# Rebuilding the opening stage of a two-layer conditioned FFN kernel on one core

## The chip, the cores and the metric

The kernel runs on one core of one Trainium2 chip, in one launch. The metric is device time in microseconds; the three runs of the kernel before gave 229.94, 229.96 and 230.28 us, with a median of 229.96 us. All inputs are drawn at random and are float32.

## The reference, cut to what matters

`x` is 32 samples of 32 channels by 512 positions, and `c = cond_128` is 32 by 128. Two layers follow each other, each with a conditioning part and an FFN part, each added to its input:

```python
# layer 0, conditioning: grouped conv over the positions, plus one number for each (sample, channel)
out  = conv1d(x, weight, groups=4, kernel=9) + (c @ c_weight.T)[:, :, None] + fside[None, :, None]
# layer 0, FFN
shared = relu(out @ up_w)**2 @ down_w
s      = top2(out @ gate_w).sum(-1)
routed = ((out @ fc1_w) @ expert_w) * s @ fc2_w
x = x + layernorm(shared + routed) * gamma + beta
# layer 1, conditioning: attention over 8 kernels, one 32x32 matrix and one bias row for each sample
h = gelu(c @ W0 + b0); h = gelu(h @ W1 + b1); att = softmax(h @ W2 + b2)
agg_w = einsum('bk,koi->boi', att, weight); agg_b = att @ bias_k
y = einsum('boi,bih->boh', agg_w, x) + agg_b[:, :, None]
# layer 1, FFN: dense W plus eight low-rank experts, weighted by a softmax of q.k
x = x + y @ W.T + b + combined(softmax(q.k), y @ A, Bm)
```

## The kernel before, in words

The work is tiled into 8 tiles (T = 0 to 7) of four samples each, 128 rows of 512 positions; layer 0 works in two halves (h = 0, 1) of four tiles. The program is written by hand: each engine has its own list of instructions, in order, and semaphores are the only order between engines. Almost every product of the FFN is done as three fp32r matmuls (`mm3`, L1121 to L1123) on operands split into a high part (made by ScalarE) and a low part (made by VectorE, for some weights by GpSimd); a float32 matmul shows as two passes in the trace.

Opening, in TensorE's order: the conv weights are turned into `wconv` (transposes at L1293; VectorE writes the mask product `wc_pad` before it at L907 and the copy out of PSUM after it at L913); the conditioning rows are turned into `cT` and `cwT` (L1299, L915); `conv(0)` and `conv(1)` (L1133); `turn_expert` (L1283); two `ones_r` matmuls on each half of `prod0` that give `B0`, the conditioning number of every (sample, channel) on all 128 partitions (L1313); the first layer of the attention MLP (L1318); `conv(2)`, `conv(3)`; the second MLP layer; the fold of `expert_w` and `fc2_w` into one matrix `ex` by twelve `mm3` matmuls (L1121 to L1123 with operands `ex_lo`, `dn_lo`); the logits (L1337). Then the up chunks begin.

For a conv of tile T, VectorE and ScalarE first make shifted copies of `x` in `XS` (`shift_copies(i)`: part 0 is tile 0, part 1 is tile 1, part 2 is tiles 2 and 3, part 3 is the second half; VectorE does 10 of 16 pieces of a part, ScalarE 6; L437, L438). `add_ctx(T)` (L808) adds `B0` to the conv result; `split_H(T)` makes `H_hi` (ScalarE L618) and `H_lo` (VectorE L818), the operands of the up chunks. `split_up(c)` makes the parts of up chunk c (ScalarE L609, VectorE L798). `B0` comes from `prod0` on GpSimd (L520), its split (ScalarE L663, VectorE L920), and an add of `fsb`, the side vector, on VectorE (L929). GpSimd's two large memsets, `gate_hl` and `BD`, stand behind `prod0` in its list (L523, L524).

A half h: up chunks 0 and 1 on the first two tiles, chunk 0 on the other two, `gate_rows`, chunk 1 on the other two, `gate_logits`, up chunk 2 (it waits for `s_R`, the split of chunk 0's squared result, L849), `scale_rows` (it waits for `diag`, VectorE L839 and ScalarE L640), two `latent`, and then eight down chunks with `up(c+3)` between them. In half 0 the transposed attention (`turn_att`, L1341), `mixing` (the 32x32 matrices of all samples, L1349) and `mixing_bias` (L1359) stand between the up chunks; VectorE turns the matrices (L979) and GpSimd writes them into the block-diagonal `BD` (L543). `mix(T)` (L1243) uses `BD` in the last down chunks of half 1 and after. Half 1 begins with `conv(4)` to `conv(7)`.

SyncE issues nearly all loads in one list: x part 0, `c_nat`, x parts 1 and 2, `fsb`, `exraw`, seven small tensors of the attention MLP, `wk`, `fc2`, `gate`, the first half of `up_raw`, `fc_raw`, the second half, two halves of `dn_raw`, x part 3, `gamma`, `rowb`, and 32 block loads of the q and k weights. ScalarE's queue carries two loads, `wc_nat` and `cw_nat`.

## Time and profile before

| | |
|---|---|
| median of three runs | 229.96 us |
| the profiled execution: its span | 228.5 us |
| TensorE matmul busy | 217.1 us, 95% |
| VectorE busy | 134.6 us, 59% |
| ScalarE busy | 85.0 us, 37% |
| GpSimd busy | 62.0 us, 27% |
| the chain that ended last, by engine | PE 87%, DVE 9%, DMA 1%, ACT 1% |
| DMA engines, mean busy share in the first eighth of the span | 0.5 to 0.9 and above |

The profiler's page gives for the profiled execution its span alone; the median of the runs lies 1.46 us above that span, and this difference is taken as what lies around the program. PE is TensorE, PEld its weight loads, DVE is VectorE, ACT is ScalarE, POOL is GpSimd, SP is SyncE, and an engine's name with a q is its queue of issued DMAs. "Idle before" in a row is the time for which an engine had nothing to do ahead of that group, with what ended it.

### The profile page before, as it was taken

The page shows a single profiled execution, that of the slowest core. Times are in us where ns is not written, and L with a number is a line of the kernel's source. Part 1 is how long each engine was busy: PE and PEld are TensorE (multiplying, and loading weights), DVE is VectorE, ACT ScalarE, POOL GpSimd, SP SyncE. Part 2 cuts the span into 40 slices and gives each one's busy share as a digit, 9 for nine tenths or more (in the row PEclk, how much of TensorE's full clock was granted, in tenths as well). Part 3 has the DMA queues.
Part 4 walks back from the last instruction along what each step waited for, and adds up shares of the span by engine and source line. Part 5 has one row for each costly group of instructions (what it writes and reads, how often), then busy time and mean ns, then how long its engine had stood idle before and what let it go on. Part 6 is the DMA issues. An engine that isn't in the chain of part 4 may idle for free.

```text
span 228.5 us, 3173 instructions
## 1 busy us (share of the span) xinstructions
PE 217.1 (95%) x1181; PEld 186.1 (81%) x1181; DVE 134.6 (59%) x279; ACT 85.0 (37%) x165; POOL 62.0 (27%) x72
## 2 busy tenths in 40 slices
PE   2787999999999999999999999999999999999994
PEld 2777886788788888999888888888998998999982
DVE  4998589876943334957462113445997555435442
ACT  6946576745954441123531013442112211211110
POOL 2504022545146643206300002442262220122000
PEclk9999999999999999999999999999999999999999
DMA  5999944200000000007526000000000110110103
GB/s 141 258 392 390 317 59 68 34 0 0 0 3 0 0 0 0 3 0 116 84 35 75 17 3 1 0 0 0 3 0 0 46 49 0 47 46 3 46 4 135
DMA packets 30400, 13.56 MB, mean 59 GB/s; under 512 B 24936, under 2 KB 25512, under 8 KB 30384
## 3 DMA queue, kind: packets, MB, share of 16 engines
q1 hardware_dynamic: 30288, 13.33, 22.2%
q8 instruction: 9, 0.15, 0.3%
q14 instruction: 7, 0.06, 0.1%
q10 hardware_dynamic: 96, 0.03, 0.1%
HBM read 11.26 MB, written 2.10 MB: 58 GB/s over the span
## 4 chain that ended last, share of the span: by engine, by line
PE 87%; DVE 9%; DMA 1%; ACT 1%; issue 0%
PE PS L1121 25%; PE PS L1122 25%; PE PS L1123 24%; PE PS L1133 7%; DVE XS L437 5%; PE PS L1243 3%; DVE up_lo L798 2%; DMA wc_nat<-in_L_cond_weight_dram 1%; DVE H_lo L920 1%; DVE dn_lo L972 0%; ACT fc_hi L690 0%; PE PS L1147 0%; PE PS L1146 0%; PE PS L1272 0%; PE PS L1359 0%
## 5 line engine op out<-in xcount | busy, mean ns | idle before, releaser
L845 DVE TENSOR_TENSOR PS<-PS,relu 128x512 f32<-128x512 f32 x16 | 11.1, 693 | 32.4 <-ACT relu L624 32.4
L1121 PE MATMUL PS<-H_hi,up_hi 128*128 128x512 f32 (+1 forms) x80 | 28.3, 354 | 0.0
L1122 PE MATMUL PS<-H_lo,up_hi 128*128 128x512 f32 (+1 forms) x80 | 27.9, 349 | 0.0
L1123 PE MATMUL PS<-H_hi,up_lo 128*128 128x512 f32 (+1 forms) x80 | 27.8, 347 | 0.0
L1133 PE MATMUL PS<-wconv,XS 128*128 128x128 f32 x192 | 25.0, 295 | 2.0 <-DVE wconv L913 1.5
L1133 PEld LDWEIGHTS PS<-wconv,XS 128*128 128x128 f32 x192 | 24.3, 210 | 2.5 <-DVE wconv L913 1.6
L1121 PE MATMUL PS<-qkT_hi,H_hi 128*128 128x320 f32 x64 | 20.3, 317 | 0.1
L1122 PE MATMUL PS<-qkT_lo,H_hi 128*128 128x320 f32 x64 | 19.8, 309 | 0.0
L1123 PE MATMUL PS<-qkT_hi,H_lo 128*128 128x320 f32 x64 | 19.8, 309 | 0.0
L624 ACT ACTIVATE relu<-PS 128x512 f32<-128x512 f32 x16 | 9.5, 597 | 25.1 <-PE PS L1123 25.1
L570 POOL TENSOR_TENSOR X<-X,rowb 128x512 f32<-128x512 f32 x8 | 10.3, 1288 | 31.3 <-PE PS L1243 31.3
L437 DVE COPY XS<-X 32x128 f32<-32x128 f32 (+2 forms) x40 | 18.1, 454 | 0.5
L1122 PE MATMUL PS<-dn_lo,ring 128*128 128x512 f32 x44 | 17.5, 399 | 0.0
L1121 PE MATMUL PS<-dn_hi,ring 128*128 128x512 f32 x44 | 17.4, 396 | 0.0
L1121 PEld LDWEIGHTS PS<-H_hi,up_hi 128*128 128x128 f32 x80 | 15.1, 189 | 2.7 <-issue 0.4
L1123 PE MATMUL PS<-dn_hi,ring 128*128 128x512 f32 x44 | 17.3, 392 | 0.0
L1123 PEld LDWEIGHTS PS<-H_hi,up_lo 128*128 128x128 f32 x80 | 15.1, 189 | 2.1
L1122 PEld LDWEIGHTS PS<-H_lo,up_hi 128*128 128x128 f32 x80 | 15.1, 189 | 2.0
L438 ACT ACTIVATE XS<-X 32x128 f32<-32x128 f32 (+2 forms) x24 | 15.8, 658 | 0.6 <-DMA X<-in_x_dram 0.3
L532 POOL TENSOR_TENSOR dn_lo<-dn_raw,dn_hi 128x512 fp32r<-128x512 f32 x8 | 10.3, 1289 | 17.2 <-ACT dn_hi L613 17.2
L574 POOL TENSOR_TENSOR wT_lo<-qk_raw,wT_hi 128x512 fp32r<-128x512 f32 x4 | 5.1, 1292 | 36.2 <-ACT wT_hi L658 36.2
L1121 PE MATMUL PS<-wT_hi,H_hi 128*128 128x512 f32 x32 | 13.1, 409 | 0.0
(189 smaller groups left out, 476.5 us busy)
## 6 DMA issues: line engine op xcount, KB each, us to landing
up_raw<-in_L_ffn_up_w_dram SPq DMA_DIRECT2D x2, 1024.0 KB, 8.0
dn_raw<-in_L_ffn_down_w_dram SPq DMA_DIRECT2D x2, 1024.0 KB, 12.9
out_dram<-X SPq DMA_DIRECT2D x8, 256.0 KB, 2.0
X<-in_x_dram SPq DMA_DIRECT2D x1, 1024.0 KB, 15.2
XS<-in_L_ffn_W_dram SPq DMA_DIRECT2D x16, 64.0 KB, 2.3
X<-in_x_dram SPq DMA_DIRECT2D x2, 256.0 KB, 3.4
X<-in_x_dram SPq DMA_DIRECT2D x1, 512.0 KB, 5.4
fc<-in_L_ffn_fc_w_dram SPq DMA_DIRECT2D x1, 512.0 KB, 3.6
```

The lines of the kernel that those rows point to most:

```text
L437: return nc.vector.tensor_copy(dst, src)
L438: return nc.scalar.activation(dst, src, ACT.Copy)
L532: nc.gpsimd.tensor_tensor(dn_lo[:, c, :], dn_raw[:, c, :], dn_hi[:, c, :].bitcast(F32), ALU.subtract).then_inc(s_dn, 1)
L570: nc.gpsimd.tensor_tensor(X[:, T, :], X[:, T, :], rowb[:], ALU.add).then_inc(s_x1b, 1)
L574: nc.gpsimd.tensor_tensor(wg_dst(g, False), wg_turned(g), wg_dst(g, True).bitcast(F32), ALU.subtract)\
L624: nc.scalar.activation(relu[:], U[i % 2], ACT.Relu).then_inc(s_relu, 1)
L845: nc.vector.tensor_tensor(U[i % 2], U[i % 2], relu[:], ALU.mult).then_inc(s_sq, 1)
L1121: nc.tensor.matmul(o, lh, rh, start=start, stop=False)
L1122: nc.tensor.matmul(o, lh, rl, start=False, stop=False)
L1123: return nc.tensor.matmul(o, ll, rh, start=False, stop=stop)
L1133: last = nc.tensor.matmul(conv_bank(T)[:, s * P:(s + 1) * P], XS[:, T % TPH * SPT + s, a:a + P], wconv[:, a], start=(a == 0), stop=(a == N ...
L1243: last = nc.tensor.matmul(mix_bank(T)[:, p, :], X[:, T, p * P:(p + 1) * P], BD[:, T], start=True, stop=True)
```

## The change

Four things change together. (1) GpSimd no longer makes `prod0` or `fc2_lo`, so its memsets run at once. (2) The conditioning numbers: TensorE multiplies `cT` by `cwT` in float32 (32x32), VectorE adds `fs32`, the side vector, ScalarE's queue stores the 4 KB to DRAM (`ctx_rows`) and loads them back, broadcast to 128 partitions, as `B0` (512 KB). (3) The fold of `expert_w` and `fc2_w` is done by four float32 matmuls (`expert_latent`) instead of twelve fp32r ones with splits, between `conv(1)` and `conv(2)`; `turn_expert` goes ahead of `conv(0)`. (4) The attention MLP and the mixing move: MLP layers and logits to down chunks 1, 3 and 5 of half 0, the softmax to the end of half 0, `mixing_bias` and `mixing` between the convs of half 1, and their results go through DRAM (`aggb_rows`, `agg_rows`) into `B1` and `BD`. Six float32 matmuls on `ones` (`warm(6)`) stand at the head of TensorE's list. The order of the loads, of the shifted copies of part 0, and of the splits is changed with it.

```diff
@@ SyncE @@
             load_x(0)
-            sp.dma_start(c_nat[:], cond_128).then_inc(ld_c, 16)
+            sp.dma_start(exraw[:], L0_ffn_expert_w.rearrange("(c p) m -> p c m", p=P)).then_inc(ld_ex, 16)
             load_x(1)
+            sp.dma_start(fc2[:], L0_ffn_fc2_w.rearrange("(c p) l -> p c l", p=P)).then_inc(ld_fc2, 16)
             load_x(2)
-            sp.dma_start(fsb[:], fside_S_0.partition_broadcast(P)).then_inc(ld_fs, 16)
...
+            sp.dma_start(fs32[:], fside_S_0.partition_broadcast(N)).then_inc(ld_fs, 16)
...
+            sp.dma_start(wk[:], L1_cond_weight.rearrange("k o i a -> k o (i a)")).then_inc(ld_wk, 16)
+
+            sp.wait_ge(s_E2p, LC)
+            for dst, src in ((W0, L1_cond_W0), (W1, L1_cond_W1), (W2, L1_cond_W2), (bk, L1_cond_bias_k)):
+                sp.dma_start(dst, src).then_inc(ld_cond, 16)
...
+            sp.wait_ge(s_agg, 2)
+            sp.dma_start(agg_rows.rearrange("n i o -> n (i o)"), agg).then_inc(st_agg, 16)
+            sp.wait_ge(st_aggb, 16)
+            sp.wait_ge(st_agg, 16)
+            sp.dma_start(B1[:], aggb_rows.rearrange("n o -> (n o)").partition_broadcast(P)).then_inc(ld_B1, 16)
+            for s in range(SPT):
+                sp.dma_start(BD[C * s:C * (s + 1), :, C * s:C * (s + 1)], blocks[s]).then_inc(ld_BD, 16)
@@ GpSimd @@
-            pool.wait_ge(s_cT, 1)
-            nc.gpsimd.tensor_tensor(prod0[:], bcast_mid(cwT[:], N), cT[:].unsqueeze(2).broadcast_to([CD, N, C]),
-                                    ALU.mult).then_inc(s_prod0, 1)
-            nc.gpsimd.tensor_tensor(fc2_lo, fc2[:], fc2_hi.bitcast(F32), ALU.subtract).then_inc(s_fc2, 1)
-            for s in range(SPT):
-                nc.gpsimd.tensor_copy(BD[C * s:C * (s + 1), :, C * s:C * (s + 1)],
@@ ScalarE @@
+            act.dma_start(c_nat[:], cond_128).then_inc(ld_c, 16)
...
-            for i in range(3):
-                shift_copies(i)
...
+            shift_copies(0)
+            act.wait_ge(s_wcT, 1)
+            nc.scalar.activation(wconv[:].rearrange("p a q -> p (a q)"), M[1][:, 0:NWIN * P], ACT.Copy)\
+                .then_inc(s_wconv, 1)
+            act.wait_ge(s_ctx, 1)
+            act.dma_start(ctx_rows, ctx_sb[:]).then_inc(st_ctx, 16)
+            shift_copies(1)
+            act.wait_ge(st_ctx, 16)
+            act.dma_start(B0[:], ctx_rows.rearrange("n o -> (n o)").partition_broadcast(P)).then_inc(ld_B0, 16)
             act.wait_ge(s_exTp, 1)
+            nc.scalar.activation(exT[:].rearrange("p c m -> p (c m)"), D[3], ACT.Copy).then_inc(s_exT, 1)
+            shift_copies(2)
+            split_up(0)
             split_H(0)
...
+            def mixing_rows():
+                for b in range(2):
+                    act.wait_ge(s_AGp, b + 1)
+                    nc.scalar.activation(agg[:, b * BANK:(b + 1) * BANK], M[b][0:N, :], ACT.Copy).then_inc(s_agg, 1)
@@ VectorE @@
-            shift_copies(0)
-            dve.wait_ge(s_wcT, 1)
-            nc.vector.tensor_copy(wconv[:].rearrange("p a q -> p (a q)"), M[1][:, 0:NWIN * P]).then_inc(s_wconv, 1)
+            dve.wait_ge(ld_x[0], 16)
+            for j in range(PH):
+                phase_copy(nc.vector, 0, j, *XPARTS[0])
+            for j in range(PH):
+                phase_copy(nc.vector, 1, j, *XPARTS[0])
             dve.wait_ge(s_cTp, 1)
             nc.vector.tensor_copy(cT[:], M[0][:, 0:N])
             nc.vector.tensor_copy(cwT[:], M[0][:, N:N + C]).then_inc(s_cT, 1)
+            for j in range(2):
+                last = phase_copy(nc.vector, 2, j, *XPARTS[0])
+            last.then_inc(xs_v, 1)
+            dve.wait_ge(ld_fs, 16)
+            dve.wait_ge(s_ctxp, 1)
+            nc.vector.tensor_tensor(ctx_sb[:], M[0][0:N, 2 * C:3 * C], fs32[:], ALU.add).then_inc(s_ctx, 1)
             shift_copies(1)
             shift_copies(2)
+            split_up(0)
             add_ctx(0)
@@ TensorE @@
                 if T == TPH + 2:
-                    pe.wait_ge(s_lat, LC)
+                    pe.wait_ge(s_agg, 2)
...
+            pe.wait_ge(s_ones, 1)
+            warm(6)
             pe.wait_ge(s_ident, 2)
...
+            turn_expert()
+            pe.wait_ge(s_cT, 1)
+            nc.tensor.matmul(M[0][0:N, 2 * C:3 * C], cT[:], cwT[:], start=True, stop=True).then_inc(s_ctxp, 1)
...
-            turn_expert()
...
+            expert_latent()
             pe.wait_ge(xs_v, 3)
             pe.wait_ge(xs_a, 3)
             conv(2)
             conv(3)
...
+                    conv(TPH)
+                    mixing_bias()
+                    conv(TPH + 1)
+                    mixing()
+                    conv(TPH + 2)
+                    conv(TPH + 3)
...
+                    if h == 0 and c == 1:
+                        hidden1()
+                    if h == 0 and c == 3:
+                        hidden2()
+                    if h == 0 and c == 5:
+                        logits()
+                if h == 0:
+                    turn_att()
```

The new `expert_latent` waits for `exT` and `fc2`, then runs, for each of two output banks, two float32 matmuls of 128x512, and raises `s_E2p`; `warm(n)` runs n float32 matmuls of 128x128 on `ones` into a PSUM bank that nothing reads.

## Rows read from the trace of the kernel before

**Rows 1.** The page's first part: busy time, share of the span and instructions.
```profile
PE 217.1 (95%) x1181; PEld 186.1 (81%) x1181; DVE 134.6 (59%) x279; ACT 85.0 (37%) x165; POOL 62.0 (27%) x72
```

**Rows 2.** Windows: stretch, its us, busy us (instructions) by engine, PEclk, DMA share, GB/s.
```profile
7.33:13.28 5.95, 5.48 (x24) 5.19 (x24) 5.77 (x13) 5.81 (x11) 3.38 (x4) 1.00 0.95 281
13.28:19.75 6.47, 4.61 (x34) 4.22 (x35) 5.96 (x13) 2.20 (x3) 1.35 (x1) 1.00 1.04 395
19.75:25.34 5.59, 5.59 (x54) 5.59 (x52) 4.13 (x7) 2.66 (x4) 1.03 (x1) 1.00 1.05 388
25.34:28.54 3.20, 3.20 (x18) 2.40 (x16) 2.09 (x6) 2.98 (x5) 0.00 (x0) 1.00 1.22 265
28.54:40.26 11.72, 11.55 (x71) 8.71 (x69) 10.88 (x21) 8.47 (x18) 2.95 (x2) 1.00 0.42 64
40.26:91.00 50.74, 50.74 (x220) 41.05 (x220) 29.26 (x48) 26.02 (x42) 23.62 (x22) 1.00 0.02 4
91.00:101.50 10.50, 10.50 (x96) 10.50 (x95) 8.65 (x15) 1.89 (x3) 1.49 (x4) 1.00 0.01 2
```

**Rows 3.** Waits of TensorE: who waited for whom, total us, times, longest.
```profile
PE PS L1313 <- DVE H_lo L920: 1.9, 1, 1.9
```

**Rows 4.** The chain of waits (start, us, what), then GpSimd's timeline over the same time.
```profile
7.78 3.23 DVE XS L437
...
7.55 1.99 POOL L520 TENSOR_TENSOR prod<-cwT,cT 128x1024 f32<-128x1024 f32 x1 [5.14 <-DVE cwT L916]
9.98 0.95 POOL L524 MEMSET BD<- 128x1024 f32 x1
```

**Rows 5.** VectorE: timeline (start, us, engine, line, operation), then one from the chain.
```profile
3.94 2.74 DVE L437 COPY XS<-X 32x128 f32<-32x128 f32 x10
...
13.26 0.39 DVE XS L437
```

**Rows 6.** ScalarE's timeline in the opening: shifted copies, small and large, a table load.
```profile
4.91 0.86 ACT L438 ACTIVATE XS<-X 32x128 f32<-32x128 f32 x2
9.53 1.99 ACT L438 ACTIVATE XS<-X 32x256 f32<-32x256 f32 x3
20.00 1.28 ACT L670 ACT_TABLE_LOAD   x1 [1.68 <-PE PS L1318]
```

**Rows 7.** SyncE's timeline (one issue); DMA issues (KB, us to landing); one window.
```profile
2.63 0.47 SPq L451 DMA_DIRECT2D fsb<-in_fside_S_dram  x1
...
X<-in_x_dram SPq DMA_DIRECT2D x1, 512.0 KB, 5.4
fsb<-in_fside_S_dram SPq DMA_DIRECT2D x1, 16.0 KB, 5.1
cw_nat<-in_L_cond_c_weight_dram ACTq DMA_DIRECT2D x1, 16.0 KB, 2.4
gamma<-in_L_ffn_ln_gamma_dram SPq DMA_DIRECT2D x1, 256.0 KB, 12.0
...
10.00:12.00 2.00, 2.00 (x12) 2.00 (x11) 1.95 (x5) 1.96 (x4) 0.93 (x2) 1.00 0.88 266
```

**Rows 8.** TensorE's timeline: the first MLP layer and the mixing, both float32.
```profile
19.62 0.30 PE L1318 MATMUL PS<-cT,W 128*128 128x32 f32 x2
...
33.24 1.90 PE L1349 MATMUL PS<-wk,attT 8*32 8x512 f32 x4
```

**Rows 9.** Timeline of VectorE, GpSimd and ScalarE ahead of up chunk 2 and scale_rows.
```profile
33.53 3.82 DVE L798 TENSOR_TENSOR up_lo<-up_raw,up_hi 128x512 fp32r<-128x512 f32 x3 [0.15 <-ACT up_hi L609]
...
33.06 2.54 POOL L528 TENSOR_TENSOR fc_lo<-fc_raw,fc_hi 128x1024 fp32r<-128x1024 f32 x1 [12.28 <-ACT fc_hi L690]
...
41.59 1.28 ACT L640 ACTIVATE lat_hi<-ident,ssum_lo 128x128 fp32r<-128x128 f32 x4 [1.81 <-DVE ssum_lo L837]
```

**Rows 10.** Timeline at the start of half 1: ScalarE's first split, VectorE's first norm.
```profile
95.87 0.63 ACT L618 ACTIVATE H_hi<-tf 128x512 fp32r<-128x512 f32 x1 [9.20 <-DVE tf L808]
...
89.00 0.70 DVE L882 BATCH_NORM_STATS2 st<-PS 128x6 f32<-128x512 f32 x1 [3.00 <-PE PS L1123]
```

More of the change, by code:

```diff
@@ L704, in _ @@
                 if h:
[L705 to L706 removed]
+                    split_H(TPH)
+                    mixing_rows()
+                    for T in range(TPH + 1, TILES):
+                        split_H(T)
                 up_relu(i0)
```

300 lines of the change are left out of this document (117 added, 183 removed).

## The prediction, made before the changed kernel ran

> **What bounds the kernel now.** I read the page's busy times first: TensorE is busy 217.1 of 228.5 us, so nothing moves the end but TensorE's own passes or its idle time [rows 1]. Then the windows, cut where TensorE's work changes [rows 2]. TensorE issues its first conv pass at 7.33 us and its first up matmul at 28.54 us. Between these lie four convs (96 passes), the turned expert weight, B0, the fold, and idle time: 0.5 us before 13.28 and 1.86 us in the stage to 19.75. From 28.54 on it is full (50.74 of 50.74 us in the window from 40.26 to 91, 10.50 of 10.50 in the convs of half 1 [rows 2]), with 0.17 us of idle ahead of 40.26. So a microsecond taken from TensorE's list, or from its waits ahead of 28.54, is a microsecond of the end, as long as no other engine becomes late. The waits name the large one: B0's matmul waits 1.9 us for the split of prod0 [rows 3]. The chain of waits names why VectorE was late for conv(1): one small shifted copy took 3.23 us, where its ten neighbours took 0.27 each, and it spans GpSimd's prod0 and its memsets, from 7.55 to 10.93 [rows 4, 5]. I read that as VectorE being held off by GpSimd.
>
> **Part 1, up to conv(0).** The memsets of gate_hl and BD (0.5 and 0.95 us [rows 4]) now run from about 2.4 to 3.9, so they can hold up the mask product at 3.36 by 0.6 us instead of a copy by 3. VectorE then makes 8 copies (2.2 us), cT and cwT (0.3), 2 copies (0.55): 4.0 + 0.6 + 3.05 = 7.65. ScalarE has one more DMA to issue (0.4), 6 copies at 0.43 (2.6 [rows 6]) and the wconv copy, 7.0. conv(0) starts near 7.75 instead of 7.33. conv passes cost 5.59 us for 48 in the fourth stage of rows 2, 0.117 each, and 5.48 for 24 in the second, 0.228 each: conv(0) ran at the lower of TensorE's two levels (1.2 GHz), though the PEclk column says 1.00, and conv(1) and all after it at 2.4. With warm(6) and the other early passes I expect the change of level inside conv(0), which ends at 10.5 to 13; it doesn't matter, for the next step is later.
>
> **Part 2, the wait for fs32.** This is what I expect to eat most of the opening's gain. In the new VectorE list the side vector is waited for ahead of shift_copies(1), and ScalarE waits for the result (s_ctx) ahead of its own shift_copies(1). fs32 is in SyncE's list behind x part 2, as fsb was, but exraw (256 KB) and fc2 (512 KB) have been put ahead of it. fsb was issued at 2.63 and landed 5.1 us later, at 7.73; x part 2, ahead of it, 5.4 us after its issue at about 2.15: they landed together, so SyncE's loads come home in order [rows 7]. At the 266 GB/s of the window from 10 to 12 us, 768 KB more are 2.95 us; at the 395 of the third stage, 2.0 [rows 2, 7]. The seven small loads no longer mix in. I take 2.5: fs32 at 10.25, between 9.7 and 10.7. Then: add 0.3 (10.55); ScalarE issues the store (0.45) and makes 6 copies (2.65): 13.7. VectorE's ten end at 13.3. conv(1) starts at 13.75, 0.5 us later than before. Queued behind the waiting instruction on VectorE are the 20 copies of parts 1 and 2, on ScalarE the store, 12 copies and the exT copy.
>
> **Part 3, conv(1) to the up chunks.** conv(1) 2.8 (16.55). The fold is right behind it: exT is copied by 14.8. It has no row in float32; the nearest is mixing, 1.90 us for 4 passes of 512 columns [rows 8], so 8 passes are 3.7 (bound below: fp32r passes of 12 in 3.20 us, 2.1 for 8; above, the lower level, 7.3; I take 3.7, the same kind of operation). It ends at 20.25, conv(2) and conv(3) at 25.85, where before the up chunks began at 28.54. Gain: 2.65 us. In other words, of TensorE's old list 1.9 of idle, 1.1 of B0, 0.6 of turn_expert and 0.3 of MLP go, 0.6 net is lost on the fold, 0.5 on the start.
> Beside it, who could be late: ScalarE, from 13.7, the B0 issue (0.45), exT (0.6), six large copies at 0.66 (4.0 [rows 6]) and split_up(0): 19.35. VectorE's large copies (10 at 0.39 [rows 5]) end at 17.2, its split_up(0) at 20.0. Then two add_ctx and two split_H, to 22.6, and split_up(1), to 23.2. The up chunks at 25.85 have 2.6 us to spare. B0 must be there at 20.0. It is issued on ScalarE's queue at 13.7 (the store, issued at 10.6, must have landed; cw_nat on that queue took 2.4 us while megabytes of SyncE's were queued [rows 7]). 512 KB at half of 390 GB/s are 2.7 us, and I add 1.5 of cw_nat's 2.4 us for the way there and back: 4.2, that is 17.9. Bounds: 2.4 us (that row) and 12 us (gamma, a broadcast in SyncE's own crowded queue). I take 4.2, by the row on ScalarE's queue.
> The Trainium skill (DMA: Bandwidth & Descriptors, on arbitration) says that each DMA engine takes turns between the queues of different issuers, packet by packet; cw_nat's 2.4 us against fsb's 5.1 agrees.
>
> **Part 4, up to scale_rows.** TensorE loses from the stage of 11.72 us [rows 2]: turn_att 0.12, mixing 1.85 [rows 8], mixing_bias and its wait 1.25. Gain: 3.2 us. But up(2) waits for VectorE's split of chunk 0, and here VectorE gets late. add_ctx(3) can only start when conv(3) ends, now just ahead of the up chunks and not 3.2 us ahead. From 25.85 (A): add_ctx(3), split_H(3), the gate's low part, two ex_lo: A + 3.3. Three split_up: 3.82 us as before, since GpSimd's fc_lo falls on them again [rows 9]: A + 7.1. Square, ScalarE's split, VectorE's split: A + 9.2. TensorE is ready for up(2) at A + 11.72 - 3.2 - 0.17 = A + 8.35. Stall: 0.9 us (0.3 if fc_lo misses them, 1.5 if ex_lo slips). Likewise scale_rows waits for the diagonals: 1.95 us of small operations and 1.28 [rows 9] behind that split, against 2.8 of up(2): 0.45.
>
> **Part 5, what comes back later.** MLP layers and logits in the down chunks: three at 0.15, 0.45 us [rows 8]. Their ScalarE work is two Gelus and a table load of 1.28 [rows 6], at chunks 4 and 6, where ScalarE idles over 1 us each time: covered. The softmax ends near 88.8 by the old clock, just ahead of VectorE's norm at 89.00 [rows 10]; add_ctx(4) has microseconds of slack if it slips. Half 1: turn_att 0.12, mixing_bias 0.13, mixing 1.85 on TensorE, and conv(6) now waits until ScalarE has copied the second mixing bank out: 0.6 and two handovers, 0.75. ScalarE is free, its first split at 95.87 [rows 10] is done before. Cost 2.85. The up chunks after the convs have their H by then. BD and B1 go out and in within some 6 us, 45 us ahead of mix(0) and y_bias(0); the W loads wait for the last conv anyway. Costed at nothing.
>
> **Sum.** -2.65 - 3.2 + 0.9 + 0.45 + 0.45 + 2.85 = -1.2 us. Span 228.5 - 1.2 = 227.3; with the 1.46 us by which the median of the runs lies above the span, 228.8. The forecast's own range, by the bounds of the fs32 landing (-0.5, +0.5) and the stalls (-0.8, +0.7), is 227.6 to 229.8.
>
> **Rivals.**
> (a) *fs32 isn't held up.* If small loads overtake, VectorE goes on at 7.65, copies of part 1 end at 11.0 (ScalarE), and conv(1) starts when conv(0) ends, about 11.5: 2.25 us less, 226.5. For it: small loads occupy little; against it: fsb landed with x part 2 [rows 7]. Chance 0.17.
> (b) *The clock falls: slower.* In my forecast TensorE idles 1 to 3 us between conv(0) and conv(1), and if the early passes don't lift it before, the change of level comes late. If conv(1) runs at the lower level it costs 5.2 and not 2.8: +2.4, 231.2. It decides from 12 slow passes on (1.2 us over 0.1 each), half of conv(1). Against it: idle of 1.86 us around 17.5 left TensorE at the higher level; for it: after the 1.5 us of idle ahead of 7.33, conv(0) was slow throughout [rows 2]. Chance 0.17.
> The Trainium skill (TensorE: Matmul & The Clock Gate, the clock gate's part) says that the array wakes after sustained activity and falls back after idleness, with a phase that is not the kernel's. By that rule warm(6) is undone by a long wait for fs32; the time would be that of (b).
> (c) *B0 is late.* At gamma's 12 us B0 lands at 26.2; add_ctx, two splits and handovers put the up chunks at 28.8, 2.9 late: 231.7. It decides from a landing at 22.6 + 1.2 = 23.8. Chance 0.08.
> (d) *The gain is absorbed*: TensorE's list gets shorter, yet VectorE's chain to up(2) sets the pace and its stall is 2 us and more. 230.0. Chance 0.08.
> My forecast has the other 0.5.
>
> **How the numbers follow.** A difference under 0.2% (0.46 us) can hardly be measured here. Faster: 0.43 of the forecast's 0.5, and (a): 0.6. Same: 0.07 of the forecast and (d): 0.15. Slower: (b), (c): 0.25. The range leaves out half of (a)'s and (b)'s far sides and (c): 226.4 to 231.2.
>
> **What would show it.** In the new profile: a wait of VectorE of 2 to 3 us for fs32's load near 8 us, and one of ScalarE beside it; conv(1) starting at 13.4 to 14; the first up matmul at 25.3 to 26.5; a TensorE wait for VectorE's L849-split of 0.3 to 1.5 us ahead of up(2); one of 0.75 for the agg copy ahead of conv(6). If the first up matmul comes before 24, part 2 is wrong; if B0's landing releases add_ctx(0), part 3 is; if TensorE is idle for over 2 us between there and scale_rows, part 4 is.

## The result, and the profile after

The changed kernel takes 235.5 us (median of 4 runs, 234.9 to 235.6) against 230.0 (229.9 to 230.3) for the kernel before: ratio 1.021, 95% interval 1.017 to 1.025. The span grew from 228.5 to 233.8 us, by 5.3. The same kernel comes out at several times, the one before at about 230.2 us with a mean granted clock of 1.00 or at 231.8 with 0.993, as if some executions had one more stretch at TensorE's lower level; medians and like-for-like pairs are compared below with that in mind.

The page of the changed kernel: busy times, and the clock granted to TensorE in 40 slices of 5.8 us.

```profile
PE 223.1 (95%) x1185; PEld 188.4 (81%) x1185; DVE 125.0 (53%) x271; ACT 83.1 (36%) x164; POOL 54.6 (23%) x66
...
PEclk9999997999999999979999999999999999999998
```

Only four more matmul passes than before, yet 6.0 us more of busy TensorE: on the whole the passes got longer, not the list [rows 1]. Two slices at 7 tenths of the clock were not there before; the last slice is the end of the program. Windows of the changed kernel, cut where TensorE's work changes (columns as in [rows 2]), say where it happened:

```profile
7.71:12.94 5.23, 4.05 (x26) 3.89 (x25) 3.19 (x13) 2.56 (x6) 0.00 (x0) 1.00 1.04 395
12.94:19.90 6.96, 6.55 (x33) 4.20 (x33) 3.38 (x9) 4.65 (x8) 0.00 (x0) 1.00 1.05 393
19.90:25.25 5.35, 5.35 (x49) 5.35 (x49) 4.48 (x7) 2.40 (x5) 0.00 (x0) 1.00 1.05 391
25.25:36.04 10.79, 8.40 (x63) 7.67 (x62) 8.42 (x12) 7.25 (x14) 2.41 (x1) 1.00 0.51 87
36.04:88.97 52.93, 52.93 (x224) 42.48 (x225) 29.20 (x55) 28.45 (x47) 21.15 (x18) 0.97 0.06 9
88.97:95.01 6.04, 6.04 (x52) 5.71 (x51) 5.86 (x11) 1.00 (x3) 1.49 (x4) 1.00 0.02 3
95.01:99.28 4.27, 3.60 (x5) 0.38 (x5) 0.80 (x2) 1.23 (x3) 0.00 (x0) 0.94 0.00 0
99.28:106.17 6.89, 6.89 (x49) 6.89 (x50) 2.08 (x3) 1.10 (x2) 0.00 (x0) 0.79 0.45 114
106.17:229.48 123.31, 123.22 (x664) 106.67 (x662) 63.28 (x147) 29.80 (x71) 26.60 (x28) 1.00 0.14 29
229.48:233.80 4.32, 0.00 (x0) 0.00 (x0) 0.69 (x1) 0.00 (x0) 0.00 (x0) 0.78 0.33 123
```

The same later stages in the kernel before: up chunk 2 to the first conv of half 1, the four convs, the rest of TensorE's work, and the end:

```profile
40.26:90.91 50.65, 50.65 (x220) 40.96 (x220) 29.17 (x48) 26.02 (x42) 23.62 (x22) 1.00 0.02 4
90.91:101.54 10.63, 10.63 (x97) 10.63 (x96) 8.74 (x15) 1.89 (x3) 1.49 (x4) 1.00 0.01 2
101.54:225.33 123.79, 123.70 (x665) 106.86 (x663) 63.22 (x147) 29.72 (x71) 26.60 (x28) 1.00 0.14 29
225.33:228.50 3.17, 0.00 (x1) 0.00 (x0) 0.69 (x1) 0.00 (x0) 0.00 (x0) 1.00 0.44 165
```

Set side by side, with what was forecast for each:

| stage | before | after | difference | forecast |
|---|---|---|---|---|
| to the first up matmul | 28.54 | 25.25 | -3.3 | -2.65 |
| from there to up chunk 2 | 11.72 | 10.79 | -0.9 | -2.3 |
| up chunk 2 to half 1 | 50.65 | 52.93 | +2.3 | +0.9 |
| half 1: convs, attention, mixing | 10.63 | 17.20 | +6.6 | +2.85 |
| the up chunks of half 1 to the last matmul | 123.79 | 123.31 | -0.5 | 0 |
| last matmul to the end | 3.17 | 4.32 | +1.15 | 0 |
| sum | 228.5 | 233.8 | +5.3 | -1.2 |

So the opening gained more than was forecast, and more than all of it was given back from 34 us on, in four places: the stall ahead of up chunk 2, the stage behind it, half 1, and the end. The waits of TensorE show two pieces of this:

```profile
PE PS L1107 <- DVE ring L856: 2.2, 1, 2.2
...
PE PS L1119 <- ACT B L701: 0.7, 1, 0.7
```

The first is the stall ahead of up chunk 2 (forecast 0.9), the last the wait of conv(6) for the mixing's copy (forecast 0.75). Timeline of the opening of the changed kernel (start, us, engine, line, operation, idle time before and its releaser): TensorE, then VectorE and ScalarE.

```profile
7.71 4.05 PE L1119 MATMUL PS<-wconv,XS 128*128 128x128 f32 x24
12.94 2.92 PE L1119 MATMUL PS<-wconv,XS 128*128 128x128 f32 x24 [1.18 <-ACT XS L433]
15.79 3.70 PE L1282 MATMUL PS<-fc,exT 128*128 128x512 f32 x8
19.90 5.60 PE L1119 MATMUL PS<-wconv,XS 128*128 128x128 f32 x48 [0.41 <-ACT XS L433]
...
9.59 0.18 DVE L931 TENSOR_TENSOR ctx_sb<-PS,fs 32x32 f32<-32x32 f32 x1 [2.20 <-DMA fs<-in_fside_S_dram]
```

conv(0) starts at 7.71 (forecast 7.75), VectorE waits 2.20 us for the side vector, conv(1) starts at 12.94 (forecast 13.75) and takes 2.92 us, and the float32 fold takes 3.70 us, as forecast. Timeline of the changed kernel ahead of up chunk 2: ScalarE, VectorE, GpSimd, TensorE.

```profile
27.75 1.06 ACT L674 ACTIVATE ex_hi<-PS 128x512 fp32r<-128x512 f32 x2
...
28.47 1.28 DVE L949 TENSOR_TENSOR ex_lo<-PS,ex_hi 128x512 fp32r<-128x512 f32 x2
29.67 0.68 DVE L805 TENSOR_TENSOR up_lo<-up_raw,up_hi 128x512 fp32r<-128x512 f32 x1
30.83 3.10 DVE L805 TENSOR_TENSOR up_lo<-up_raw,up_hi 128x512 fp32r<-128x512 f32 x2 [0.48 <-ACT up_hi L602]
...
30.37 2.41 POOL L530 TENSOR_TENSOR fc_lo<-fc_raw,fc_hi 128x1024 fp32r<-128x1024 f32 x1 [26.59 <-ACT fc_hi L677]
...
36.04 0.47 PE L1107 MATMUL PS<-H_hi,up_hi 128*128 128x512 f32 x1 [2.19 <-DVE ring L856]
```

And TensorE around the mixing:

```profile
95.01 3.59 PE L1344 MATMUL PS<-wk,fc 8*32 8x512 f32 x4
99.28 7.01 PE L1119 MATMUL PS<-wconv,XS 128*128 128x128 f32 x48 [0.68 <-ACT B L701]
```

The mixing takes 3.59 us where it took 1.90 before [rows 8], and conv(6) and conv(7) take 7.01 where 48 conv passes took 5.59 [rows 2]. Last, DMA issues of the changed kernel (KB, us from issue to landing):

```profile
B<-ctx_rows ACTq DMA_DIRECT2D x1, 512.0 KB, 6.4
fs<-in_fside_S_dram SPq DMA_DIRECT2D x1, 4.0 KB, 6.4
ctx_rows<-ctx_sb ACTq DMA_DIRECT2D x1, 4.0 KB, 4.9
```

The trip of the conditioning rows through DRAM took 4.9 + 6.4 us; the forecast had the store landed within 3.1 us, by a row of 2.4, and 4.2 for the load.

### The profile page after: what moved, and what is told of

Its sections match the earlier page's. It is cut to its first block, busy times and chain, and to the rows that moved or that the text cites. A ratio compares the mean times of both kernels' runs of the same rounds, so it can differ in the third digit from the quotient of the medians.

```text
span 233.8 us, 3164 instructions
## 1 busy us (share of the span) xinstructions
PE 223.1 (95%) x1185; PEld 188.4 (81%) x1185; DVE 125.0 (53%) x271; ACT 83.1 (36%) x164; POOL 54.6 (23%) x66
## 3 DMA queue, kind: packets, MB, share of 16 engines
q1 hardware_dynamic: 31472, 14.10, 22.2%
## 4 chain that ended last, share of the span: by engine, by line
PE 82%; DMA 5%; ACT 5%; DVE 4%; issue 1%; SPq 1%; ACTq 0%; DVEq 0%
PE PS L1107 24%; PE PS L1109 23%; PE PS L1108 23%; PE PS L1119 5%; PE PS L1226 3%; DMA fs<-in_fside_S_dram 3%; DMA ctx_rows<-ctx_sb 2%; DVE up_lo L805 2%; ACT XS L433 2%; PE PS L1344 2%; DVE tf L815 1%; ACT up_hi L602 1%; SPq L440 1%; ACT H_hi L611 1%; DVE H_lo L825 1%
## 5 line engine op out<-in xcount | busy, mean ns | idle before, releaser
L1109 PE MATMUL PS<-H_hi,up_lo 128*128 128x512 f32 (+1 forms) x80 | 28.4, 355 | 0.0
L1119 PE MATMUL PS<-wconv,XS 128*128 128x128 f32 x192 | 25.5, 296 | 2.3 <-ACT XS L433 1.6
L534 POOL TENSOR_TENSOR dn_lo<-dn_raw,dn_hi 128x512 fp32r<-128x512 f32 x8 | 10.3, 1293 | 22.9 <-ACT dn_hi L606 22.9
L432 DVE COPY XS<-X 32x128 f32<-32x128 f32 (+2 forms) x40 | 15.1, 378 | 0.5
L856 DVE TENSOR_TENSOR ring<-PS,ring 128x512 fp32r<-128x512 f32 x11 | 7.6, 692 | 10.8 <-ACT ring L623 10.8
```

Source lines behind the costliest of these rows:

```text
L432: return nc.vector.tensor_copy(dst, src)
L534: nc.gpsimd.tensor_tensor(dn_lo[:, c, :], dn_raw[:, c, :], dn_hi[:, c, :].bitcast(F32), ALU.subtract).then_inc(s_dn, 1)
L856: nc.vector.tensor_tensor(R_lo[i % NR], U[i % 2], R_hi[i % NR].bitcast(F32), ALU.subtract).then_inc(s_R, 1)
L1109: return nc.tensor.matmul(o, ll, rh, start=False, stop=stop)
L1119: last = nc.tensor.matmul(conv_bank(T)[:, s * P:(s + 1) * P], XS[:, T % TPH * SPT + s, a:a + P], wconv[:, a], start=(a == 0), stop=(a == N ...
```

## The experiments

The theory after reading the two traces: the opening worked; the loss is (i) the mixing's operand, read with a stride, (ii) ScalarE's and VectorE's splits ahead of up chunk 2, (iii) the clock, which falls after the thin or idle places, and (iv) something at the end. The rivals: that the wait for `fs32` is what counts, that TensorE's new `warm` and the clock's history count, or that the moved work as such costs this much. Each edit is on the changed kernel, except where it says the kernel before. Where a text gives the time of a fall of the clock, it is the start of the low stretch in the granted clock; the passes grow longer some 0.3 us behind it, which is what the expectations call 37.7 and 99.1.

**The mixing's operand in stored order.** `wk` is stored as (k, o, i), and the changed kernel reads it as (k, i, o), neighbours 32 elements apart; here it is read as stored, and ScalarE's copy does the permuting.

```diff
-                wf = wk[:].rearrange("k o i -> k i o")
+                wf = wk[:].rearrange("k o i -> k (o i)")
...
-                    nc.scalar.activation(agg[:, b * BANK:(b + 1) * BANK], M[b][0:N, :], ACT.Copy)
+                    rows = agg.rearrange("n (i o) -> n o i", o=C)[:, b * C // 2:(b + 1) * C // 2, :]
+                    nc.scalar.activation(rows, M[b][0:N, :].rearrange("n (o i) -> n o i", i=C), ACT.Copy)
```

> The changed kernel with one edit: the mixing matmuls read wk in its stored order (k, o, i), and ScalarE's copy out of PSUM turns the rows to (i, o) instead. In the changed kernel each of the four mixing passes took 0.86 us where the same shape took 0.46 before, and the granted clock fell to half at 99.1 us, just behind them. Theory (the strided operand is what makes the passes slow): the four passes take 1.85 us again, 1.75 less, and with less idle-looking time ahead of conv(6) the half-clock stretch there (1.4 us of loss) may go too: 1.75 to 3.2 us faster than the changed kernel, so 232.3 to 233.8. Rival (the passes were slow because TensorE was at its lower level there, or because of their eight rows): they stay at 0.86 and the time stays at 235.5.

Measured: 235.5 us (234.2 to 236.6, 4 runs), before 231.7 beside it (12 runs, 230.0 to 232.0), ratio 1.019 (1.012 to 1.026). The timeline of TensorE:

```profile
95.71 1.90 PE L1345 MATMUL PS<-wk,fc 8*32 8x512 f32 x4
98.72 8.54 PE L1121 MATMUL PS<-wconv,XS 128*128 128x128 f32 x48 [1.11 <-ACT B L702]
```

The four passes are back at 1.90 us: the stride is what doubled them. The rival that they were slow because of the lower clock is out for another reason too: in the changed kernel the clock fell at 98.8, after they had ended. But nothing came of it in the time. ScalarE's copies now take 0.94 us each instead of 0.59, so conv(6) waits 1.11, and conv(6) and (7) take 8.54 us, the lower clock lasting from 98.0 to 104.9. The size of (i) is shown, and that (iii) can eat it. The long low stretch isn't this edit's own: in the nine profiles with the mixing between the convs, conv(6) and (7) took 7.0 to 7.3 us in four and 7.4 to 8.5 in five, three of these with no edit near the mixing.

**The side vector first.** `fs32` is loaded right behind part 0 of x.

```diff
+            sp.dma_start(fs32[:], fside_S_0.partition_broadcast(N)).then_inc(ld_fs, 16)
...
-            sp.dma_start(fs32[:], fside_S_0.partition_broadcast(N)).then_inc(ld_fs, 16)
```

> The changed kernel with one edit: the 4 KB load of fs32 stands right behind x part 0 in SyncE's list instead of behind x part 2. Theory (VectorE's 2.2 us wait for fs32 held up conv(1)): fs32 lands near 4 to 5 us, ctx_sb is made at 7.6, conv(1) starts when conv(0) ends, near 11.8 instead of 12.94, and B0 lands about 2 us earlier; the first up matmul comes 1 to 1.5 us earlier, at 24. What that is worth at the end depends on the stall ahead of up chunk 2: if the splits move with it, 1 to 2 us, 233.5 to 234.5. Rival (the stall ahead of up(2) takes it all, for its chain starts from conv(3), ScalarE and GpSimd): no change, 235.5.

Measured: 234.2 us (232.3 to 234.7, 4 runs), ratio 1.013 (1.006 to 1.019), 1.1 us less than the changed kernel in its second set (235.3, below), with ranges that overlap. conv(0) and conv(1) run back to back from 7.18 to 14.26, the fold begins at 14.10 and not at 15.79; but the stall ahead of up chunk 2 stays 2.2 us. The first up matmul comes at 22.9 instead of 25.25, and 1.6 us of that are left at up chunk 2 (34.41 for 36.04): VectorE now waits 0.79 us for B0, and TensorE stands 0.92 us among the first up chunks. The time lies in the range of the theory. The wait for `fs32` is real and worth about 1 us, but its end isn't where the loss of the changed kernel went.

**The splits moved.** ScalarE makes `fc_hi` right behind its second set of copies; `ex_hi` goes behind the first relu, and `ex_lo` behind VectorE's gate sum.

```diff
             act: shift copies of part 1
+            act.wait_ge(ld_fc, 16)
+            nc.scalar.activation(fc_hi[:], fc_raw[:], ACT.Copy).then_inc(s_fch, 1)
...
+                        nc.scalar.activation(ex_hi[:, i, :], D[i], ACT.Copy).then_inc(s_E2h, 1)
...
+                        nc.vector.tensor_tensor(ex_lo[:, i, :], D[i], ex_hi[:, i, :].bitcast(F32),
+                                                ALU.subtract).then_inc(s_E2, 1)
```

> The changed kernel with the splits off the way to up chunk 2: fc_hi goes behind shift_copies(1) on ScalarE (so that GpSimd's fc_lo meets other VectorE work), and ex_hi, ex_lo go behind the first relu and the gate sum. Theory (the 2.19 us stall ahead of up(2) is VectorE's queue: ex_lo 1.2 us and the hold-off by fc_lo about 2, and the half-clock stretch from 37.7 to 41.1 us is a follow-up of that idle time): the stall goes to 0.3 or less, the half-clock stretch with it (1.6 us): 3 to 3.8 us faster, 231.7 to 232.5. Rival (the chain is ScalarE's, relu and two splits): the stall goes down by 0.5 at most, the half-clock stretch stays, 235.

Measured: 233.7 us (232.1 to 234.6, 9 runs), ratio 1.010 (1.006 to 1.013). VectorE and TensorE in this run:

```profile
28.17 1.89 DVE L805 TENSOR_TENSOR up_lo<-up_raw,up_hi 128x512 fp32r<-128x512 f32 x3
...
33.74 0.47 PE L1108 MATMUL PS<-H_hi,up_hi 128*128 128x512 f32 x1 [0.21 <-DVE ring L856]
```

Three splits take 1.89 us instead of 0.68 + 3.10, because GpSimd's `fc_lo` no longer falls on them and `ex_lo` isn't ahead of them. The stall goes from 2.19 to 0.21, the clock doesn't fall there, and `scale_rows` waits 0.7 us, where it waited 0.4 with the stall and no fall. The theory of the stall holds; in the time the edit is worth 1.6 us against the second set of the changed kernel, half of the 3 to 3.8 that were expected. The fall behind the mixing stays, at 96.7.

**TensorE kept busy in the stall.** Nine float32 matmuls on `ones` ahead of up chunk 2, adding no number to any result.

```diff
+                if h == 0:
+                    for _ in range(9):
+                        nc.tensor.matmul(D[3][:, 0:P], ones[:], ones[:], start=True, stop=True)
```

> The changed kernel with nine float32 matmuls of 128x128 on ones (18 passes, 2.1 us) issued ahead of up chunk 2, in the time in which TensorE otherwise waits 2.19 us. Their result isn't read. Theory (the idle time itself brings the half-clock stretch that follows): up(2) starts within 0.2 us of where it did, the stretch at the half clock is gone and 1.5 us with it: 234.0. Rival (the fall of the clock has another cause, or a phase of its own): it stays, and the time is 235.5 to 235.7.

Measured: 234.7 us (234.3 to 235.0, 4 runs), ratio 1.016 (1.011 to 1.021). The filling passes, and the window from up chunk 2 on:

```profile
34.01 2.27 PE L1366 MATMUL PS<-ones 128*128 128x128 f32 x18
...
36.00:40.00 4.00, 3.62 (x17) 2.59 (x16) 3.46 (x14) 1.69 (x5) 1.30 (x1) 1.00 0.44 68
```

The same stretch in the changed kernel:

```profile
36.04:40.92 4.88, 4.88 (x15) 3.85 (x15) 3.21 (x12) 1.42 (x5) 1.30 (x1) 0.65 0.44 69
```

The granted clock is 1.00 with the fill and 0.65 without it; up chunk 2 starts no earlier (36.27). One execution each would prove little, as the next run shows. But over the profiles of the changed kernel and its variants: with the stall of 2.2 us the clock fell at or behind it in five of nine, with the stall filled or down to 0.2 us in none of five. These are few, and point one way without settling it.

**The changed kernel again**, for a profile of its own.

> The changed kernel itself, run again beside the others, since the kernel before was seen at two times 1.7 us apart (230.1 and 231.8) in the last comparison, with a mean granted clock of 1.0 and 0.993. If these are one stretch at the half clock more or less, the changed kernel should also show two or more times, 1 to 2 us apart, around 235.5.

Measured: 235.3 us (234.5 to 236.9, 4 runs), before 230.4 (17 runs), ratio 1.023 (1.018 to 1.028). Two windows of this profile:

```profile
36.00:41.00 5.00, 4.62 (x20) 3.49 (x20) 2.98 (x11) 2.39 (x7) 1.28 (x1) 1.00 0.45 70
99.00:103.00 4.00, 4.00 (x24) 4.00 (x23) 0.77 (x2) 0.00 (x0) 0.00 (x0) 0.57 0.57 164
```

The same stall of 2.19 us, and the clock did not fall behind it; the fall at 99 came again. So the stall doesn't decide a fall; at most it opens a chance of one. The pair prices the fall at 37.4: from up chunk 2 to the mixing took 58.97 us with it and 57.99 without, so 1.0 us. The longer passes cost 1.4; without them TensorE waits 0.38 us for `scale_rows`' diagonals, a wait (forecast 0.45) that the slow passes of the first profile hid. The kernel before may have such falls too, in its executions with a mean of 0.993; at what place no trace shows.

**The end.** 24 more waits of SyncE that are satisfied already, behind its wait for the first finished tile.

```diff
+                if T == 0:
+                    for _ in range(24):
+                        sp.wait_ge(s_fin, 1)
```

> The changed kernel with 24 more (already satisfied) waits in SyncE's list behind its first wait for a finished tile; no other engine is touched. In the kernel before, the span ended 2.4 us after VectorE's last operation, in the changed kernel and its first four variants 3.6 us after it, and an 8 KB instruction fetch lies in the last microsecond of these. Theory (SyncE's own instructions are being fetched at the end, because its list now reaches the next block there): the fetch moves ahead, into the time in which SyncE waits, and the end is 2.4 us behind VectorE again: 1.2 us faster than the changed kernel. Rival (another engine's list, or the order of the DMA queues): it stays at 3.6.

Measured: 235.7 us (233.6 to 236.5, 4 runs), ratio 1.021. SyncE's own wait in the changed kernel, and it is the same here:

```profile
SPq L103 <- DMA out_dram<-X: 2.8, 1, 2.8
```

It was 1.7 in the kernel before. The fetch of instructions didn't move either: it lies 1.8 us ahead of the end, 1.7 in the changed kernel. So the edit didn't do what it was made for, and the theory that the code's place decides is neither shown nor excluded.

**The mixing late.** `mixing_bias` and `mixing` (stored order) go behind down chunks 1 and 2 of half 1, their copies and the DRAM trip with them. conv(6) no longer waits for a copy.

```diff
-                    mixing_bias()
...
-                    mixing()
...
+                    if h and c == 1:
+                        mixing_bias()
+                    if h and c == 2:
+                        mixing()
```

> The changed kernel with mixing_bias and mixing (operand in stored order) moved from between the convs of half 1 to behind the down chunks 1 and 2 of half 1, and their stores and loads behind the load of the last bias. TensorE's work stays the same but for the four passes at 0.46; conv(6) waits for nothing new. Theory (the mixing between the convs cost its strided passes, 1.75 us, the wait for ScalarE, 0.7 to 1.1, and a stretch at the half clock, 1.4 or more): all three go, 3.8 to 4.5 us faster than the changed kernel, near 231.5 where it gives 235.5; the half-clock stretch ahead of scale_rows stays. Rival (a thin matmul of 8 rows and 32 columns lowers the clock wherever it stands): a stretch at the half clock follows the mixing in the down chunks, and 1.4 us or more of the gain is missing.

Measured: 230.55 us (230.0 to 231.65, 10 runs), ratio 0.999 (0.996 to 1.002), 4.8 us less than the changed kernel. In the timeline the mixing takes 1.90 us at 139, and the page shows no slice behind the opening that loses the clock:

```profile
139.03 1.90 PE L1349 MATMUL PS<-wk,fc 8*32 8x512 f32 x4
...
PEclk9799999999999999999999999999999999999999
```

The list of TensorE is as long as in the first experiment (235.5); the place differs, and with it conv(6)'s wait. So with the operand in stored order the place of the mixing among the convs, with its copy and what it does to the clock, costs about 5 us, most of the loss. The profiles of all variants agree: with the mixing between the convs the clock fell within it or less than 2 us behind it in nine of nine, with the mixing late in none of five.

**The mixing late, with the strided operand**, as the pair to that.

> The kernel with the late mixing, but with the operand turned while it is read, as in the changed kernel: the four thin passes take 3.6 us in the middle of the full down chunks, with no idle time of TensorE around them. Theory B (the thin passes themselves lower the clock when there are enough of them together): a stretch at the half clock begins during them or right behind them, and the kernel is 1.75 us (passes) plus 1.5 to 2.5 us slower than the late mixing in stored order, 233.5 to 234.5. Theory A (it takes idle time beside them): no stretch at the half clock, 1.75 us slower, 232.3.

Measured: 234.2 us (232.1 to 235.7, 4 runs; before 231.3), ratio 1.013 (1.006 to 1.020). The profiled execution, the fastest of them, shows only the stride's price:

```profile
138.11 3.60 PE L1348 MATMUL PS<-wk,fc 8*32 8x512 f32 x4
...
138.10:141.70 3.60, 3.60 (x6) 0.44 (x5) 2.19 (x4) 1.66 (x3) 0.00 (x0) 1.00 0.00 0
```

Its mean clock was 0.996, its span 230.3. The other three had means of 0.978 to 0.985 and took 1.7 to 3.6 us more; where their low stretches lay can't be told, since they have no trace. A mean alone doesn't tell the price: the kernel with the stored order took 230.2 us in an execution with 0.985, and its profile shows a low stretch in the opening, ahead of a wait. Against its 230.55 the strided operand costs 3.7 us, 1.7 of which are its own passes; the cause of the rest is not shown. The median lies in the range of theory B, the profile agrees with theory A; falls behind the thin passes in the untraced three are possible and not seen.

The four kernels together: between the convs 235.3 to 235.5 with the stride and 235.5 in stored order; late 234.2 with the stride and 230.55 in stored order. Stored order alone brings nothing, the late place alone 1.1 us, both 4.8.

**The mixing's gap filled.** Three float32 matmuls on `ones` between the mixing and conv(6).

```diff
+                    for _ in range(3):
+                        nc.tensor.matmul(D[0][:, 0:P], ones[:], ones[:], start=True, stop=True)
```

> The changed kernel with three float32 matmuls of 128x128 on ones (6 passes, 0.7 us) between mixing and conv(6), in the time in which TensorE waits 0.68 us for ScalarE; their result isn't read. Theory A (the idle time is what lowers the clock ahead of conv(6)): the half-clock stretch after the mixing is gone, 1.4 us faster. Theory B (the thin passes of 8 rows and 32 columns, 3.6 us of them, count for little): the stretch stays and the time is unchanged.

Measured: 235.1 us (232.8 to 235.7, 4 runs), ratio 1.018 (1.012 to 1.023). Timeline and windows around it:

```profile
94.82 3.59 PE L1344 MATMUL PS<-wk,fc 8*32 8x512 f32 x4
98.34 1.65 PE L1357 MATMUL PS<-ones 128*128 128x128 f32 x6
99.78 7.44 PE L1119 MATMUL PS<-wconv,XS 128*128 128x128 f32 x48
...
94.80:98.30 3.50, 3.50 (x5) 0.38 (x4) 0.82 (x2) 0.59 (x1) 0.00 (x0) 0.81 0.00 0
```

No idle time is left, and the granted clock still falls, at 97.0, inside the strided passes, with TensorE busy for all of the 3.50 us. In three more profiles of the nine it fell inside them, at 95.6, 96.2 and 97.4. So idle time isn't needed. That it is the thin passes (8 rows by 32 columns of the array) is the reading left, but no run changes their width alone. The last of the four strided passes began at 97.38, below the fall, and took as long as the others (1.03 us from its start to its modelled end): the lower level cost it nothing. Of the three untraced executions one took 232.8 us with a mean clock of 0.989; what was different in it isn't known.

**No warming passes.** `warm(6)` and its wait are left out.

```diff
-            pe.wait_ge(s_ones, 1)
-            warm(6)
```

> The changed kernel without the six float32 matmuls on ones at its head. Theory (the wait for fs32 hides conv(0), so warm(6) buys nothing here): conv(0) takes 5.1 us instead of 4.05 and ends at 12.8, conv(1) starts at 13.0 as before, unless the change to the higher level comes after it, which would cost up to 2.4: the time is that of the changed kernel, 234.5 to 236.9, within its own spread. Rival (warm(6) sets when the level rises and so the later course): slower by 1 us or more.

Measured: 234.5 us (234.3 to 235.5, 4 runs), ratio 1.018 (1.014 to 1.021). conv(0) starts at 7.51 and takes 4.54 us instead of 4.05, conv(1) starts at 12.81 instead of 12.94. But with the warming passes conv(0) took anything from 3.84 to 4.80 us in the other profiles, so the half microsecond isn't shown to be theirs, and it lies ahead of a wait for the copies: the warming passes buy nothing.

**Memsets first, alone, on the kernel before.**

```diff
-            pool.wait_ge(s_cT, 1)
-            nc.gpsimd.tensor_tensor(prod0[:], ...)
             (memsets of gate_hl and BD)
+            pool.wait_ge(s_cT, 1)
+            nc.gpsimd.tensor_tensor(prod0[:], ...)
```

> The kernel before with one edit: its three memsets (nhalf, gate_hl, BD) stand ahead of prod0 in GpSimd's list, as in the changed kernel; all else is as before. Theory (GpSimd holds VectorE off while it writes): the shifted copy that took 3.23 us from 7.78 takes 2.0 or less, since only prod0 (1.99 us) is in its way; the mask product at 3.4 may lose 0.5. VectorE's chain to B0 gets 0.7 to 1.3 us shorter, and so does the kernel, 229.0 at the higher of its two clock states' shares. Rival (the copy was long for another reason, such as its load): no change.

Measured: 228.9 us (12 runs) against 230.3 (17 runs), ratio 0.994 (0.992 to 0.997); of the executions at full clock 228.8 against 230.2. VectorE's copies, GpSimd's memset and product in the timeline, and one copy from the chain of waits:

```profile
7.36 8.40 DVE L437 COPY XS<-X 32x128 f32<-32x128 f32 x20
...
2.83 0.95 POOL L521 MEMSET BD<- 128x1024 f32 x1
7.41 1.99 POOL L523 TENSOR_TENSOR prod<-cwT,cT 128x1024 f32<-128x1024 f32 x1 [3.64 <-DVE cwT L916]
...
7.63 1.89 DVE XS L437
```

The 20 copies took 9.7 us before. The blocked copy takes 1.89 us instead of 3.23: it still ends with `prod0`, but no longer with the memsets behind it, and these 1.3 to 1.4 us reach the end. The mask product, which the prediction had held up by 0.6 us beside the early memsets, took 0.65 us with them and without. The Trainium skill (SBUF — State Buffer, "SBUF: two separate sides") calls the port pair of VectorE and GpSimd an exclusive lock, held for a whole instruction; 1.89 us beside a product of 1.99, against 0.27 for the same copy alone, agrees.

**All of it together**: late mixing in stored order, moved splits, side vector first.

> The changed kernel with four edits together: fs32 loaded behind x part 0, fc_hi and the two ex splits off the way to up chunk 2, mixing in stored order and in the down chunks of half 1. Theory (the losses are separate and add up): the first up matmul near 23.7, no stall over 0.5 us ahead of up(2) or conv(6), no half-clock stretch in the middle: 233.8 - 2.8 (splits) - 3.8 (mixing) - 1.3 (fs32) is a span of 225.9, so about 227.5, 1% faster than the kernel before. Rival (the waits hide each other, so that the edits don't add): 229 to 230.5, no better than the kernel before.

Measured: 228.2 us (227.9 to 229.1, 6 runs), ratio 0.990 (0.987 to 0.994), span 226.4.

**The same with `exT` copied first and `fc_hi` later**, to take away a 3.7 us stand of ScalarE at `fc_raw`'s load.

> The combined kernel with ScalarE's list in the opening reordered: the exT copy right behind shift_copies(1), then the wait for the store of ctx_rows and the load of B0, shift_copies(2), and only then fc_hi. In the combined kernel ScalarE stood 3.74 us at fc_hi for its load, and TensorE 1.33 us at the fold for exT. Theory: the fold starts when conv(1) ends, at 14.4 instead of 15.7, and the convs follow it at 18.1; the first up matmul comes at 23.7 to 24.3, 1 to 1.5 us earlier: 226.8 to 227.3. Rival (B0's landing and the splits are late next): up chunks wait for add_ctx and split_H, 0 to 0.5 us of gain.

Measured: 228.65 us (227.9 to 229.1, 6 runs), ratio 0.991 (0.988 to 0.995): no gain. The convs end earlier, but `fc_lo` falls on VectorE again:

```profile
18.36 2.43 DVE L810 TENSOR_TENSOR up_lo<-up_raw,up_hi 128x512 fp32r<-128x512 f32 x1 [4.40 <-ACT up_hi L604]
```

TensorE begins its first up chunks at 23.5 and then stands 1.5 us among them, until VectorE's split for the last tile is done at 28.0. Opening earlier brought nothing here, for this split was hardly earlier (27.28 to 27.97; 27.53 to 28.22 with all edits together).

**Late mixing and moved splits, the side vector where the change put it.**

> The kernel with the late mixing and the splits off the way to up chunk 2 (fc_hi, ex_hi, ex_lo moved), fs32 still behind x part 2. In the changed kernel the splits alone gave 1.6 us and the late mixing alone 4.8. Theory (these are separate losses, and the wait for fs32 is small beside them): 228.6 to 229.2, so that of the combined kernel's gain the load of fs32 has 0.5 at most. Rival (the splits' gain needs the earlier fs32): 230.

Measured: 228.2 us (227.3 to 229.1, 6 runs), ratio 0.988 (0.984 to 0.992). TensorE's waits in it:

```profile
PE PS L1126 <- ACT XS L433: 2.2, 2, 1.8
...
PE PS L1176 <- ACT lat_hi L635: 0.7, 1, 0.7
PE PS L1113 <- DVE ring L861: 0.2, 1, 0.2
```

As fast as with the side vector first: the wait for `fs32` costs nothing here that can be measured. With the side vector first another wait had taken its place, for ScalarE stood 3.7 us at `fc_raw`'s load and TensorE 1.33 us at the fold. The moved splits are worth 2.4 us on the kernel with the late mixing (230.55, another set), where the stall they end is 2.0.

## Why the prediction was wrong

It said 228.8 (226.4 to 231.2), and 0.6 for faster; it was 235.5.

**Parts 1 to 3 held, with one landing mis-sized, and rival (a) was worth less than said.** conv(0), the wait for `fs32` and the fold came as forecast, a little early in sum: conv(1) 0.8 us earlier, the first up matmul 0.6 us earlier. The term I called the main eater of the gain, the wait for `fs32`, was there (2.20 us, landing at 9.6 for a forecast of 10.25), but taking it away brought 1.1 us alone (rival (a) had 2.25) and nothing in combination, where another wait took its place. Rival (c) didn't happen, though its term was mis-sized: B0 landed at 21.1, 3.2 us later than the forecast's 17.9. The store of the rows took 4.9 us, so ScalarE stood 2.34 us and issued the load at 14.74 and not 13.7, and the load took 6.4 us and not 4.2. It was still ahead of the 23.8 from which it decides.

**Part 4, the stall ahead of up chunk 2: right mechanism, a term mis-sized.** Forecast 0.9 (0.3 to 1.5), measured 2.19. TensorE was ready at A + 8.60 (forecast 8.35), VectorE's split ended at A + 10.65 (forecast 9.2). Of VectorE's 1.45 us, 1.2 are `ex_lo`, which ended at A + 4.5 and not 3.3. VectorE's list was behind by then: its first split of the up weights ended at 21.13 for a forecast of 20.0, since ScalarE's half of it had waited behind the late store, and its first `add_ctx` followed at 21.18, when B0 had just landed too; the later tiles went hand to hand between the two engines (two waits of 0.70 us of VectorE for `H_hi`). Another 0.48 is a wait for `up_hi`, for `fc_hi` (1.06 us) had been put ahead of it on ScalarE. The three splits themselves took 3.78 against the 3.82 of [rows 9]. So I priced VectorE's list by its own length and let ScalarE's list in front of it stand at no cost. The moved splits brought the stall to 0.2. The wait of `scale_rows` was right: 0.38 for a forecast of 0.45, in the profile in which the clock didn't fall ahead of it.

**Part 5, half 1: the step that failed.** It had 2.85 us for the mixing between the convs, and the stage grew by 6.6. Two terms of it were wrong: the mixing's passes, and the clock, which stood in the sum at nothing (next paragraph). Taking the mixing out of there, in stored order, gave 4.8 us back. For the passes it took the 1.85 us of [rows 8], from L1349 of the kernel before, where they read their operand in stored order. The changed line reads it with a stride of 32 elements, 128 bytes, and a pass of 512 columns takes 0.90 us instead of 0.475 (a quarter of 3.59 and of 1.90): 1.7 us more. The changed source line showed the stride. The contiguous version of the same passes was back at 1.90 us. The Trainium skill (Advanced Engine Details and Errata, "SBUF Cachelines") says that SBUF has 16-byte lines and that an access to another line each time is penalized; 128 bytes from element to element, and 0.90 against 0.475 us, agree with it. The wait of conv(6) was right, 0.68 for a forecast of 0.75.

**The clock: in the wrong place.** Rival (b) had the clock fall at conv(1). conv(1) ran at the higher level (2.92 us). It fell at 37.4, behind the stall, in one of the changed kernel's two profiles (1.0 us), and at 99 in both (7.01 and 7.25 us for 5.59, so 1.4 and 1.7). I asked for its risk only where TensorE is idle in the opening; the sum had no term for what the change puts into the middle of a kernel whose profiled execution had been full and at full clock from 28 to 225 us. The runs show two places: the stall of 2.2 us (a fall in five profiles of nine, none of five without it), and the thin mixing between the convs (nine of nine), where in four the clock fell with TensorE busy throughout. What about the mixing brings the fall stays open: the thin passes fit, but the same passes at 138 us had none behind them in their one profile. The Trainium skill (TensorE: Matmul & The Clock Gate, "What's actually happening") describes a gate that watches activity with a phase of its own; that the same stall had a fall behind it in one execution and not in another agrees with that.

**Late placement.** Moving the MLP layers into the down chunks cost nearly what was forecast: the stage is 1.3 us longer once the 1.0 of the clock is taken off, of a forecast 0.9 that holds the wait of `scale_rows`. "Costed at nothing" for the DRAM trips of B1 and BD holds as well: no wait of TensorE has them behind it.

**The end, 1.15 us: not in the sum, and open.** The last store lands 3.2 us after its issue and not 2.0. In the changed kernel an 8 KB fetch of instructions lies in the last two microseconds, in the kernel before none. SyncE's last wait was 2.8 to 2.9 us in both profiles of the changed kernel and nine variants of it, 2.1 in three others, 1.7 in the kernel before and in its variant. The fetch lies in the last two microseconds of the three with 2.1 as well, so its presence alone doesn't give the 2.8, and that it delays the store is not shown.

The sum, then: of the 6.5 us between -1.2 and +5.3, the stride is 1.7, the stage with the stall 1.4, the clock 2.4, the end 1.15, and small extras 1.0 (0.4 in the stage of the MLP layers, 0.6 in the convs of half 1), less 0.65 of a better opening and 0.5 in the long last stage. These are differences of single profiles, not of separate edits, and they don't come back one by one: stored order alone gave nothing. Two small slips beside them: the bounds named add up to 227.5 to 230.0 and not 227.6 to 229.8, and every execution's time lies 1.7 us above its own span, not 1.46, which makes the forecast 229.0. The change without its late losses (late mixing and moved splits, 228.2) is 1% faster than the kernel before and 0.6 us from the forecast, though not by the forecast's terms: it has no stall and no mixing between the convs, and the end's 1.15 us in it.

## What to carry to other kernels

When a diff moves an operation, compare its operands' access patterns too: the old row prices the old pattern, and a stride of 128 bytes doubled these passes. Into a stretch where the bound engine is full and at its full clock put nothing that waits, and be wary of thin passes; if such work must go there, put it where its result is not waited for: in stored order the same four passes cost about 5 us less at 139 us (230.55 against 235.5) than between two convs. Judge two such edits together too, for the stored order showed its worth only in the late place. And when an engine's stall is forecast from the list of its releaser, work out the start times in the list of the releaser's own releaser as well.

## What the runs showed of the hardware

- A float32 pass of 512 columns whose moving operand steps 128 bytes takes 0.90 us, the same in stored order 0.475. A strided pass that began after the clock had fallen took no longer than the three before it.
- The granted clock can fall while TensorE is busy without a gap: inside thin passes (8 rows, 32 columns) in four profiles, at 97.0 in one. The same passes at 138 left it alone in the one profiled execution.
- One stall of 2.2 us in nine profiles: the clock fell at or behind it in five.
- A 4 KB store to DRAM took 4.9 us while the loads ran at 390 GB/s, a 4 KB load in SyncE's full queue 6.4, and 2.4 when it was issued ahead of the large ones.
- One copy of VectorE took 3.23 us beside a product and three memsets of GpSimd, 1.89 beside the product alone, 0.27 alone; with the memsets out of the way, 1.4 us of the whole kernel came back.
